# One eight-row pass in place of two diagonal passes for the row of top-2 sums, in an fp32 FFN kernel on one core

## The chip, the core and the metric

The kernel runs on one core of one Trainium2 chip. The metric is the device time of one execution in microseconds; three runs of the kernel before gave 230.13 to 230.21 us, with a median of 230.16 us. The engines are TensorE (PE: matmuls; PEld: its weight loads), VectorE (DVE), ScalarE (ACT), GpSimd (POOL) and SyncE (SP). Each executes its own list of instructions in the order in which they are written, and they meet through semaphores.

## The reference

The input x is 32 x 32 x 512 in fp32, which makes 1024 tokens. Two residual layers are computed. The first runs a grouped convolution with a bias that depends on a condition, then a feed-forward layer whose routed branch is scaled per token by the sum of the two largest gate logits, then a layer norm. The second mixes channels by weights from a small network and applies a dense layer with eight soft-routed low-rank experts. Cut to the lines that the change concerns:

```python
logits = jnp.einsum('bsh,he->bse', hidden_states, gate_w)          # 8 experts
routing_weights, selected_experts = jax.lax.top_k(logits, K)       # K = 2
h = jax.nn.relu(jnp.einsum('bsh,hi->bsi', hidden_states, up_w)) ** 2
shared_out = jnp.einsum('bsi,ih->bsh', h, down_w)
x_latent = jnp.einsum('bsh,hl->bsl', hidden_states, fc1_w)
expert_out = jnp.einsum('bsl,lm->bsm', x_latent, expert_w)
moe_out = expert_out * jnp.sum(routing_weights, axis=-1, keepdims=True)
routed_out = jnp.einsum('bsl,lh->bsh', moe_out, fc2_w)
return _layernorm(shared_out + routed_out, ln_gamma, ln_beta)
```

## The kernel before

The tokens are cut into two halves (h = 0, 1) of four tiles (TPH = 4) of 128 tokens, so that a half is 512 tokens wide, one PSUM bank. There are eight banks: D[0..3] accumulate the output tiles, U[0..1] take the up projection, M[0..1] take everything small. In layer 1 the activations lie with features on the partitions (H_hi, H_lo: the fp32 value cut into two parts that TensorE reads as fp32r), and a product is made of three passes, hi x hi, hi x lo and lo x hi (`mm3`, lines 1121 to 1123).

The order of the work is written out by hand: each engine's block has one list of calls per half. TensorE's list in a half (lines 1363 to 1394) is: convolution, up(0) and up(1) in parts with gate_rows between them (the gate's logits as rows), gate_logits (four small transposes, line 1158), in half 0 also mixing_bias (lines 1359 and 1360), up(2), scale_rows, latent(0), latent(1), then down and up chunks by turns. `up(i)` fills bank U[i % 2]. ScalarE then makes relu of it (line 624), VectorE multiplies the bank by relu (up_square, line 845, semaphore s_sq), ScalarE copies the result to the high part R_hi (up_split, line 630, s_Rh), and VectorE makes the low part R_lo (up_split, line 849, s_R). The down chunks read R_hi and R_lo.

The scale by the top-2 sum must be multiplied into the latent activations, where tokens run along the free dimension. So the four columns of sums (`ssum`, 128 tokens x 4 tiles, one sum per partition) have to become a row of 512 values that stands on all 128 partitions. Before, this is done as follows. `gate_sum` on VectorE finds the two largest logits (line 829), adds them (line 832), rounds the sum to `ssum_hi` (line 835) and keeps the rest in `ssum_lo` (line 837, s_suml). Then VectorE makes `diag_hi`, four 128 x 128 diagonal matrices, by multiplying the identity by each column (line 839, four instructions, s_diag), and ScalarE makes `diag_lo` in the same way from `ssum_lo` (`diag_low`, line 640, four instructions, s_diagl). Both diagonals lie in the buffer lat_hi. TensorE's `scale_rows` waits for both and multiplies a matrix of ones by them in two passes of 512 columns (lines 1184 and 1185):

```python
pe.wait_ge(s_diag, h + 1)
pe.wait_ge(s_diagl, h + 1)
nc.tensor.matmul(M[0], ones_r[:], diag_hi, start=True, stop=False)
nc.tensor.matmul(M[0], ones_r[:], diag_lo, start=False, stop=True).then_inc(s_sbp, 1)
```

ScalarE copies M[0] to `sbc` (`scale_rows`, line 634), and VectorE multiplies the latent banks by it (`lat_scale`, line 856) after `latent(n)`, 12 passes each, has filled them. In half 0, VectorE's list has between gate_sum and up_square(1) the two transposes of `turn_agg` (line 979), and ScalarE's list has `make_B1` (line 700, two copies of what mixing_bias made) behind diag_low. GpSimd meanwhile makes low parts of weights (line 532) and, once turn_agg is done, four copies into BD (line 543).

Of the kernel before, what the change touches and what calls it, by code (L numbers as in the profile page):

```python
# [6 lines left out]
F32 = mybir.dt.float32  # L7
# [9 lines left out]
def bass_adaln_ffn(  # L17
# [85 lines left out]
    with ExitStack() as ctx:  # L103
# [3 lines left out]
        def sem(name):  # L107
            return ctx.enter_context(nc.semaphore(name))
# [42 lines left out]
        ssum = sb("ssum", [P, TPH])  # L151
        ssum_hi = sb("ssum_hi", [P, TPH], F32R)
        ssum_lo = sb("ssum_lo", [P, TPH], F32R)
        st6 = sb("st6", [P, 2, 6])
# [50 lines left out]

        diag_hi, diag_lo = lat_hi[:, 0], lat_hi[:, 1]

# [111 lines left out]
        s_suml = sem("s_suml")  # L319
        s_diag = sem("s_diag")  # L320
        s_diagl = sem("s_diagl")
        s_sbp = sem("s_sbp")
# [179 lines left out]
        def _(pool):  # L502
# [18 lines left out]
                                    ALU.mult).then_inc(s_prod0, 1)  # L521
            nc.gpsimd.memset(nhalf[:], -0.5)
            nc.gpsimd.memset(gate_hl[:].bitcast(mybir.dt.uint32), 0).then_inc(s_gatez, 1)
            nc.gpsimd.memset(BD[:], 0.0).then_inc(s_zero, 1)
# [72 lines left out]
        def _(act):  # L597
# [37 lines left out]

            def diag_low(h):

                act.wait_ge(s_suml, h + 1)
                for t in range(TPH):
                    last = nc.scalar.activation(diag_lo[:, t * P:(t + 1) * P], ident[:], ACT.Copy,  # L640
                                                scale=ssum_lo[:, t:t + 1].bitcast(F32))
                last.then_inc(s_diagl, 1)

            def gate_copy(h):
# [57 lines left out]
            for h in range(HALVES):  # L702
                i0 = h * IC
                if h:
                    for t in range(TPH):
                        split_H(TPH + t)
                up_relu(i0)
                if h == 0:
                    gate_copy(h)
                    up_split(i0)  # L710
                else:
                    up_split(i0)
                    gate_copy(h)
                up_relu(i0 + 1)
                if h == 0:
                    split_dn(0)
                diag_low(h)
                if h == 0:
                    make_B1()
                scale_rows(h)  # L720
                up_split(i0 + 1)
                if h == 0:
                    split_up(5)
                up_relu(i0 + 2)
                up_split(i0 + 2)
                for n in range(LC):
                    if h == 0:
                        split_dn(1 + n)
                        split_up(6 + n)
                    lat_split(h * LC + n)  # L730
                for c in range(3, IC):
                    if h == 0:
                        split_dn(c)
                    up_relu(i0 + c)
                    up_split(i0 + c)
                    if h == 0 and c == 3:
                        act.wait_ge(s_conv, TPH)
                        shift_copies(3)
                    for g in groups_after(h, c):
                        group_split(g)  # L740
# [50 lines left out]
        def _(dve):  # L791
# [29 lines left out]
            def gate_sum(h):  # L821
# [12 lines left out]
                dve.wait_ge(s_sum, h + 1)  # L834
                nc.vector.tensor_copy(ssum_hi[:], ssum[:]).then_inc(s_sumh, 1)
                dve.wait_ge(s_sumh, h + 1)
                nc.vector.tensor_tensor(ssum_lo[:], ssum[:], ssum_hi[:].bitcast(F32), ALU.subtract).then_inc(s_suml, 1)
                for t in range(TPH):
                    last = nc.vector.tensor_scalar(diag_hi[:, t * P:(t + 1) * P], ident[:],
                                                   ssum_hi[:, t:t + 1].bitcast(F32), None, ALU.mult)  # L840
                last.then_inc(s_diag, 1)

# [139 lines left out]
            for h in range(HALVES):  # L982
# [22 lines left out]
                up_square(i0 + 1)  # L1005
                up_split(i0 + 1)
                if h == 0:
                    split_up(5)
# [109 lines left out]
        def _(pe):  # L1118
# [42 lines left out]

            def up(i, part=None):

# [8 lines left out]
                if i >= 2:  # L1172
                    pe.wait_ge(s_R, i - 1)
                for p in range(PH):
                    last = mm3(U[i % 2][:, part], up_hi[:, c, p], up_lo[:, c, p], H_hi[:, p, part],
                               H_lo[:, p, part], p == 0, p == PH - 1)
                if part.stop == TOKH:
                    last.then_inc(s_upp, 1)

            def scale_rows(h):  # L1180

                pe.wait_ge(s_diag, h + 1)
                pe.wait_ge(s_diagl, h + 1)
                nc.tensor.matmul(M[0], ones_r[:], diag_hi, start=True, stop=False)
                nc.tensor.matmul(M[0], ones_r[:], diag_lo, start=False, stop=True).then_inc(s_sbp, 1)

            def latent(n):

                h, c = divmod(n, LC)
                if c == 0:  # L1190
                    pe.wait_ge(s_top, h + 1)
                else:
                    pe.wait_ge(s_sb, h + 1)
# [169 lines left out]
            for h in range(HALVES):  # L1363
# [16 lines left out]
                if h == 0:  # L1380
                    mixing_bias()
                up(h * IC + 2)
                scale_rows(h)
# [70 lines left out]
```

## Time and profile before

| what | value |
|---|---|
| median of 3 runs | 230.16 us (230.13 to 230.21) |
| the profiled execution | span 228.5 us from its first to its last instruction; the page gives no other time of it |
| TensorE busy | 217.1 us, 95% of the span |
| VectorE / ScalarE / GpSimd busy | 134.6 / 85.0 / 62.0 us |
| chain that ended last | TensorE 87%, VectorE 9%, the rest 4% |
| granted TensorE clock, mean | 1.000 |

The span covers the execution's instructions alone; the device time of a run also holds what lies around them, which is why the median is 1.7 us above the span. A matmul row's duration runs from its start to the modelled end of its results, so neighbours overlap; what one costs its engine is the distance from its start to the start of the next.

### The profile page before, as it was taken

Reading aid. Unit: us, or ns where it says so; the run is one execution under the profiler, and the core shown is the slowest. Engines: PE = TensorE matmul, PEld = TensorE weight load, DVE = VectorE, ACT = ScalarE, POOL = GpSimd, SP = SyncE. Lnnn points to the kernel's source line nnn. Section 1 sums busy time; section 2 is a strip of 40 time slices with the busy share of each in tenths; the row PEclk is TensorE's granted clock in tenths of the full one; section 3 lists DMA queues with packets and bytes.
Section 4 is the critical chain, followed back from the end, with each engine's and each line's share of the span. In section 5 each row is a group of like instructions: output and inputs, shape, how many; then the busy total and the mean of one; then the engine's idle time right before and its main releaser. Section 6 shows DMA issues by size and latency. Waiting matters only on the chain.

```text
span 228.5 us, 3173 instructions
## 1 busy us (share of the span) xinstructions
PE 217.1 (95%) x1181; PEld 186.1 (81%) x1181; DVE 134.6 (59%) x279; ACT 85.0 (37%) x165; POOL 62.0 (27%) x72
## 2 busy tenths in 40 slices
PE   2787999999999999999999999999999999999994
PEld 2777886788788888999888888888998998999982
DVE  4998589876943334957462113445997555435442
ACT  6946576745954441123531013442112211211110
POOL 2504022545146643206300002442262220122000
PEclk9999999999999999999999999999999999999999
DMA  5999944200000000007526000000000110110103
GB/s 141 258 392 390 317 59 68 34 0 0 0 3 0 0 0 0 3 0 116 84 35 75 17 3 1 0 0 0 3 0 0 46 49 0 47 46 3 46 4 135
DMA packets 30400, 13.56 MB, mean 59 GB/s; under 512 B 24936, under 2 KB 25512, under 8 KB 30384
## 3 DMA queue, kind: packets, MB, share of 16 engines
q1 hardware_dynamic: 30288, 13.33, 22.2%
q8 instruction: 9, 0.15, 0.3%
q14 instruction: 7, 0.06, 0.1%
q10 hardware_dynamic: 96, 0.03, 0.1%
HBM read 11.26 MB, written 2.10 MB: 58 GB/s over the span
## 4 chain that ended last, share of the span: by engine, by line
PE 87%; DVE 9%; DMA 1%; ACT 1%; issue 0%
PE PS L1121 25%; PE PS L1122 25%; PE PS L1123 24%; PE PS L1133 7%; DVE XS L437 5%; PE PS L1243 3%; DVE up_lo L798 2%; DMA wc_nat<-in_L_cond_weight_dram 1%; DVE H_lo L920 1%; DVE dn_lo L972 0%; ACT fc_hi L690 0%; PE PS L1147 0%; PE PS L1146 0%; PE PS L1272 0%; PE PS L1359 0%
## 5 line engine op out<-in xcount | busy, mean ns | idle before, releaser
L845 DVE TENSOR_TENSOR PS<-PS,relu 128x512 f32<-128x512 f32 x16 | 11.1, 693 | 32.4 <-ACT relu L624 32.4
L1121 PE MATMUL PS<-H_hi,up_hi 128*128 128x512 f32 (+1 forms) x80 | 28.3, 354 | 0.0
L1122 PE MATMUL PS<-H_lo,up_hi 128*128 128x512 f32 (+1 forms) x80 | 27.9, 349 | 0.0
L1123 PE MATMUL PS<-H_hi,up_lo 128*128 128x512 f32 (+1 forms) x80 | 27.8, 347 | 0.0
L1133 PE MATMUL PS<-wconv,XS 128*128 128x128 f32 x192 | 25.0, 295 | 2.0 <-DVE wconv L913 1.5
L1133 PEld LDWEIGHTS PS<-wconv,XS 128*128 128x128 f32 x192 | 24.3, 210 | 2.5 <-DVE wconv L913 1.6
L1121 PE MATMUL PS<-qkT_hi,H_hi 128*128 128x320 f32 x64 | 20.3, 317 | 0.1
L1122 PE MATMUL PS<-qkT_lo,H_hi 128*128 128x320 f32 x64 | 19.8, 309 | 0.0
L1123 PE MATMUL PS<-qkT_hi,H_lo 128*128 128x320 f32 x64 | 19.8, 309 | 0.0
L624 ACT ACTIVATE relu<-PS 128x512 f32<-128x512 f32 x16 | 9.5, 597 | 25.1 <-PE PS L1123 25.1
L570 POOL TENSOR_TENSOR X<-X,rowb 128x512 f32<-128x512 f32 x8 | 10.3, 1288 | 31.3 <-PE PS L1243 31.3
L437 DVE COPY XS<-X 32x128 f32<-32x128 f32 (+2 forms) x40 | 18.1, 454 | 0.5
L1122 PE MATMUL PS<-dn_lo,ring 128*128 128x512 f32 x44 | 17.5, 399 | 0.0
L1121 PE MATMUL PS<-dn_hi,ring 128*128 128x512 f32 x44 | 17.4, 396 | 0.0
L1121 PEld LDWEIGHTS PS<-H_hi,up_hi 128*128 128x128 f32 x80 | 15.1, 189 | 2.7 <-issue 0.4
L1123 PE MATMUL PS<-dn_hi,ring 128*128 128x512 f32 x44 | 17.3, 392 | 0.0
L1123 PEld LDWEIGHTS PS<-H_hi,up_lo 128*128 128x128 f32 x80 | 15.1, 189 | 2.1
L1122 PEld LDWEIGHTS PS<-H_lo,up_hi 128*128 128x128 f32 x80 | 15.1, 189 | 2.0
L438 ACT ACTIVATE XS<-X 32x128 f32<-32x128 f32 (+2 forms) x24 | 15.8, 658 | 0.6 <-DMA X<-in_x_dram 0.3
L532 POOL TENSOR_TENSOR dn_lo<-dn_raw,dn_hi 128x512 fp32r<-128x512 f32 x8 | 10.3, 1289 | 17.2 <-ACT dn_hi L613 17.2
L574 POOL TENSOR_TENSOR wT_lo<-qk_raw,wT_hi 128x512 fp32r<-128x512 f32 x4 | 5.1, 1292 | 36.2 <-ACT wT_hi L658 36.2
L1121 PE MATMUL PS<-wT_hi,H_hi 128*128 128x512 f32 x32 | 13.1, 409 | 0.0
(189 smaller groups left out, 476.5 us busy)
## 6 DMA issues: line engine op xcount, KB each, us to landing
up_raw<-in_L_ffn_up_w_dram SPq DMA_DIRECT2D x2, 1024.0 KB, 8.0
dn_raw<-in_L_ffn_down_w_dram SPq DMA_DIRECT2D x2, 1024.0 KB, 12.9
out_dram<-X SPq DMA_DIRECT2D x8, 256.0 KB, 2.0
X<-in_x_dram SPq DMA_DIRECT2D x1, 1024.0 KB, 15.2
XS<-in_L_ffn_W_dram SPq DMA_DIRECT2D x16, 64.0 KB, 2.3
X<-in_x_dram SPq DMA_DIRECT2D x2, 256.0 KB, 3.4
X<-in_x_dram SPq DMA_DIRECT2D x1, 512.0 KB, 5.4
fc<-in_L_ffn_fc_w_dram SPq DMA_DIRECT2D x1, 512.0 KB, 3.6
```

Of the source, the lines that this page charges most:

```text
L437: return nc.vector.tensor_copy(dst, src)
L438: return nc.scalar.activation(dst, src, ACT.Copy)
L532: nc.gpsimd.tensor_tensor(dn_lo[:, c, :], dn_raw[:, c, :], dn_hi[:, c, :].bitcast(F32), ALU.subtract).then_inc(s_dn, 1)
L570: nc.gpsimd.tensor_tensor(X[:, T, :], X[:, T, :], rowb[:], ALU.add).then_inc(s_x1b, 1)
L574: nc.gpsimd.tensor_tensor(wg_dst(g, False), wg_turned(g), wg_dst(g, True).bitcast(F32), ALU.subtract)\
L624: nc.scalar.activation(relu[:], U[i % 2], ACT.Relu).then_inc(s_relu, 1)
L845: nc.vector.tensor_tensor(U[i % 2], U[i % 2], relu[:], ALU.mult).then_inc(s_sq, 1)
L1121: nc.tensor.matmul(o, lh, rh, start=start, stop=False)
L1122: nc.tensor.matmul(o, lh, rl, start=False, stop=False)
L1123: return nc.tensor.matmul(o, ll, rh, start=False, stop=stop)
L1133: last = nc.tensor.matmul(conv_bank(T)[:, s * P:(s + 1) * P], XS[:, T % TPH * SPT + s, a:a + P], wconv[:, a], start=(a == 0), stop=(a == N ...
L1243: last = nc.tensor.matmul(mix_bank(T)[:, p, :], X[:, T, p * P:(p + 1) * P], BD[:, T], start=True, stop=True)
```

## The change

The sums' high and low parts are put side by side in `ssum_hl`, 128 tokens x 8 columns, both as plain fp32. A new `turn_sums` on TensorE, written between the second and the third of up(2)'s four steps, transposes them into 8 rows of 128 in the bank M[1]. A new `spread_sums` on VectorE, written behind up_split(1), multiplies these 8 rows, repeated four times along the free dimension, by a block mask `blocks` (8 x 4, made once on GpSimd), so that row k keeps only the 128 columns of its own tile; the result `srows` is 8 x 512. `scale_rows` on TensorE then is one pass over 8 rows with 8 rows of ones as weights. The eight diagonal instructions go. ScalarE's up_split(1) stands ahead of its scale_rows now, where it stood behind it. `latent(0)` waits for s_srows instead of s_top.

```diff
-        ssum_hi = sb("ssum_hi", [P, TPH], F32R)
-        ssum_lo = sb("ssum_lo", [P, TPH], F32R)
+        ssum_r = sb("ssum_r", [P, TPH], F32R)
+        ssum_hl = sb("ssum_hl", [P, 2, TPH])
+        blocks = sb("blocks", [2 * TPH, TPH])
...
-        diag_hi, diag_lo = lat_hi[:, 0], lat_hi[:, 1]
+        srows = lat_hi[0:2 * TPH, 0].rearrange("k (t q) -> k t q", t=TPH)
...
             nc.gpsimd.memset(nhalf[:], -0.5)
+            nc.gpsimd.memset(blocks[:], 0.0).then_inc(s_blocks, 1)
+            for i in range(2):
+                pool.wait_ge(s_blocks, i + 1)
+                nc.gpsimd.affine_select(out=blocks[:], in_=blocks[:], compare_op=ALU.not_equal, fill=1.0,
+                                        base=-i * TPH, pattern=[[-1, TPH]], channel_multiplier=1).then_inc(s_blocks, 1)
...
-            def diag_low(h):
-
-                act.wait_ge(s_suml, h + 1)
-                for t in range(TPH):
-                    last = nc.scalar.activation(diag_lo[:, t * P:(t + 1) * P], ident[:], ACT.Copy,
-                                                scale=ssum_lo[:, t:t + 1].bitcast(F32))
-                last.then_inc(s_diagl, 1)
...
                 if h == 0:
                     split_dn(0)
-                diag_low(h)
                 if h == 0:
                     make_B1()
+                up_split(i0 + 1)
                 scale_rows(h)
-                up_split(i0 + 1)
...
-                nc.vector.tensor_copy(ssum_hi[:], ssum[:]).then_inc(s_sumh, 1)
+                nc.vector.tensor_copy(ssum_r[:], ssum[:]).then_inc(s_sumh, 1)
                 dve.wait_ge(s_sumh, h + 1)
-                nc.vector.tensor_tensor(ssum_lo[:], ssum[:], ssum_hi[:].bitcast(F32), ALU.subtract).then_inc(s_suml, 1)
-                for t in range(TPH):
-                    last = nc.vector.tensor_scalar(diag_hi[:, t * P:(t + 1) * P], ident[:],
-                                                   ssum_hi[:, t:t + 1].bitcast(F32), None, ALU.mult)
-                last.then_inc(s_diag, 1)
+                nc.vector.tensor_copy(ssum_hl[:, 0], ssum_r[:].bitcast(F32))
+                nc.vector.tensor_tensor(ssum_hl[:, 1], ssum[:], ssum_r[:].bitcast(F32), ALU.subtract).then_inc(s_suml, 1)
+
+            def spread_sums(h):
+
+                dve.wait_ge(s_sumT, h + 1)
+                dve.wait_ge(s_blocks, 3)
+                nc.vector.tensor_tensor(srows, bcast_mid(M[1][0:2 * TPH, 256:256 + P], TPH),
+                                        blocks[:].unsqueeze(2).broadcast_to([2 * TPH, TPH, P]), ALU.mult)\
+                    .then_inc(s_srows, 1)
...
                 up_square(i0 + 1)
                 up_split(i0 + 1)
+                spread_sums(h)
...
-                pe.wait_ge(s_diag, h + 1)
-                pe.wait_ge(s_diagl, h + 1)
-                nc.tensor.matmul(M[0], ones_r[:], diag_hi, start=True, stop=False)
-                nc.tensor.matmul(M[0], ones_r[:], diag_lo, start=False, stop=True).then_inc(s_sbp, 1)
+                pe.wait_ge(s_srows, h + 1)
+                nc.tensor.matmul(M[0], ones_r[0:2 * TPH, :], lat_hi[0:2 * TPH, 0], start=True, stop=True)\
+                    .then_inc(s_sbp, 1)
+
+            def turn_sums(h):
+
+                pe.wait_ge(s_suml, h + 1)
+                nc.tensor.transpose(M[1][0:2 * TPH, 256:256 + P], ssum_hl[:].rearrange("p v t -> p (v t)"), ident[:])\
+                    .then_inc(s_sumT, 1)
...
                 if c == 0:
-                    pe.wait_ge(s_top, h + 1)
+                    pe.wait_ge(s_srows, h + 1)
...
-                up(h * IC + 2)
+                up(h * IC + 2, ps=range(0, 2))
+                turn_sums(h)
+                up(h * IC + 2, ps=range(2, PH))
                 scale_rows(h)
```

VectorE's list in half 0, from the end of gate_sum on, with what each instruction waits for; lat_hi is the buffer of the diagonals before and of srows now, ring is R_hi and R_lo, and M and U lie in PS. Before:

```order
L835 CAST ssum_hi<-ssum 128x4 [waits s_sum]
L837 TENSOR_TENSOR ssum_lo<-ssum,ssum_hi 128x4 [waits s_sumh]
L839 TENSOR_SCALAR lat_hi<-ident,ssum_hi 128x128 x4
L979 STREAM_TRANSPOSE prod<-PS 32x512 [waits s_AGp]
L979 STREAM_TRANSPOSE prod<-PS 32x512
L845 TENSOR_TENSOR PS<-PS,relu 128x512 [waits s_relu]
L849 TENSOR_TENSOR ring<-PS,ring 128x512 [waits s_Rh]
L798 TENSOR_TENSOR up_lo<-up_raw,up_hi 128x512 [waits s_uph]
```

In the changed kernel (its lines from there on are numbered a few apart):

```order
L833 CAST ssum_r<-ssum 128x4 [waits s_sum]
L835 COPY ssum_hl<-ssum_r 128x4 [waits s_sumh]
L836 TENSOR_TENSOR ssum_hl<-ssum,ssum_r 128x4
L982 STREAM_TRANSPOSE prod<-PS 32x512 [waits s_AGp]
L982 STREAM_TRANSPOSE prod<-PS 32x512
L848 TENSOR_TENSOR PS<-PS,relu 128x512 [waits s_relu]
L852 TENSOR_TENSOR ring<-PS,ring 128x512 [waits s_Rh]
L842 TENSOR_TENSOR lat_hi<-PS,blocks 8x512 [waits s_blocks,s_sumT]
L796 TENSOR_TENSOR up_lo<-up_raw,up_hi 128x512 [waits s_uph]
```

The four instructions that made the diagonals are gone from ahead of the two transposes, and the instruction that the last pass of scale_rows waits for now stands behind up_square(1) and behind up_split(1), which itself waits for ScalarE.

ScalarE's list in half 0, from up_relu(1) on. Before:

```order
L624 ACTIVATE relu<-PS 128x512 [waits s_sq,s_upp]
L613 ACTIVATE dn_hi<-dn_raw 128x512 [waits ld_dn0]
L640 ACTIVATE lat_hi<-ident,ssum_lo 128x128 [waits s_suml]
L640 ACTIVATE lat_hi<-ident,ssum_lo 128x128 x3
L700 ACTIVATE B<-PS 128x512 [waits s_B1p] x2
L634 ACTIVATE sbc<-PS 128x512 [waits s_sbp]
L630 ACTIVATE ring<-PS 128x512 [waits s_sq]
L609 ACTIVATE up_hi<-up_raw 128x512 [waits ld_up1]
L624 ACTIVATE relu<-PS 128x512 [waits s_sq,s_upp]
```

In the changed kernel:

```order
L631 ACTIVATE relu<-PS 128x512 [waits s_sq,s_upp]
L620 ACTIVATE dn_hi<-dn_raw 128x512 [waits ld_dn0]
L699 ACTIVATE B<-PS 128x512 [waits s_B1p] x2
L637 ACTIVATE ring<-PS 128x512 [waits s_sq]
L641 ACTIVATE sbc<-PS 128x512 [waits s_sbp]
L616 ACTIVATE up_hi<-up_raw 128x512 [waits ld_up1]
L631 ACTIVATE relu<-PS 128x512 [waits s_sq,s_upp]
```

The copy to the ring (up_split(1)) no longer stands behind the copy to sbc, and the diagonals are gone from ahead of both.

TensorE's list in half 0 around scale_rows; the rows with up_hi and up_lo are steps of up(2), the rows with fc_hi are latent(0). Before:

```order
L1121 MATMUL PS<-H_hi,up_hi 128x512
L1122 MATMUL PS<-H_lo,up_hi 128x512
L1123 MATMUL PS<-H_hi,up_lo 128x512
L1184 MATMUL PS<-lat_hi,ones_r 128x512 [waits s_diagl,s_diag]
L1185 MATMUL PS<-lat_hi,ones_r 128x512
L1121 MATMUL PS<-H_hi,fc_hi 128x512 [waits s_fc,s_top]
```

In the changed kernel:

```order
L1127 MATMUL PS<-H_hi,up_lo 128x512
L1193 MATMUL PS<-ident,ssum_hl 8x128 [waits s_suml]
L1125 MATMUL PS<-H_hi,up_hi 128x512 [waits s_R,s_up]
L1126 MATMUL PS<-H_lo,up_hi 128x512
L1127 MATMUL PS<-H_hi,up_lo 128x512
L1125 MATMUL PS<-H_hi,up_hi 128x512
L1126 MATMUL PS<-H_lo,up_hi 128x512
L1127 MATMUL PS<-H_hi,up_lo 128x512
L1187 MATMUL PS<-lat_hi,ones_r 128x512 [waits s_srows]
L1125 MATMUL PS<-H_hi,fc_hi 128x512 [waits s_fc,s_srows]
```

The wait for s_srows stands at the one pass of scale_rows, and the whole of latent(0) and latent(1) is queued behind it.

## Rows read from the trace of the kernel before

**Rows 1.** The page, part 1: the span, and TensorE's busy time and instructions.
```profile
span 228.5 us, 3173 instructions
...
PE 217.1 (95%) x1181; PEld 186.1 (81%) x1181; DVE 134.6 (59%) x279; ACT 85.0 (37%) x165; POOL 62.0 (27%) x72
```

**Rows 2.** The page, part 4: the chain that ended last, by engine.
```profile
PE 87%; DVE 9%; DMA 1%; ACT 1%; issue 0%
```

**Rows 3.** Waits of TensorE (us in total, times, longest us); five rows in all.
```profile
PE PS L1313 <- DVE H_lo L920: 1.9, 1, 1.9
...
PE PS L1359 <- DVE dn_lo L972: 0.2, 1, 0.2
```

**Rows 4.** Timeline, TensorE, first half (start us, us busy, engine, line, [idle before]).
```profile
39.14 0.49 PE L1359 MATMUL PS<-dn_lo,ones_r 8*128 8x512 f32 x1 [0.17 <-DVE dn_lo L972]
39.47 0.38 PE L1360 MATMUL PS<-dn_lo,ones_r 8*128 8x512 f32 x1
...
41.75 0.39 PE L1121 MATMUL PS<-H_hi,up_hi 128*128 128x512 f32 x1
...
43.12 0.39 PE L1184 MATMUL PS<-lat_hi,ones_r 128*128 128x512 f32 x1
...
43.58 0.40 PE L1121 MATMUL PS<-H_hi,fc_hi 128*128 128x512 f32 x1
```

**Rows 5.** Timeline, VectorE, first half.
```profile
41.39 0.16 DVE L837 TENSOR_TENSOR ssum_lo<-ssum,ssum_hi 128x4 fp32r<-128x4 f32 x1
41.47 0.87 DVE L839 TENSOR_SCALAR lat_hi<-ident,ssum_hi 128x128 fp32r<-128x128 f32 x4
42.25 1.29 DVE L979 STREAM_TRANSPOSE prod<-PS 32x512 f32<-32x512 f32 x2
43.48 0.66 DVE L845 TENSOR_TENSOR PS<-PS,relu 128x512 f32<-128x512 f32 x1
44.89 0.69 DVE L849 TENSOR_TENSOR ring<-PS,ring 128x512 fp32r<-128x512 f32 x1 [0.75 <-ACT ring L630]
...
48.60 1.42 DVE L798 TENSOR_TENSOR up_lo<-up_raw,up_hi 128x512 fp32r<-128x512 f32 x1 [0.35 <-ACT up_hi L609]
```

**Rows 6.** Timeline, ScalarE, first half.
```profile
41.59 1.28 ACT L640 ACTIVATE lat_hi<-ident,ssum_lo 128x128 fp32r<-128x128 f32 x4 [1.81 <-DVE ssum_lo L837]
42.77 1.05 ACT L700 ACTIVATE B<-PS 128x512 f32<-128x512 f32 x2
```

**Rows 7.** Timeline, GpSimd, first half.
```profile
43.69 3.12 POOL L543 COPY BD<-prod 32x256 f32<-32x256 f32 x4 [2.55 <-DVE prod L979]
```

**Rows 8.** Timeline, VectorE, second half.
```profile
106.77 0.70 DVE L845 TENSOR_TENSOR PS<-PS,relu 128x512 f32<-128x512 f32 x1 [0.34 <-ACT relu L624]
108.13 0.69 DVE L849 TENSOR_TENSOR ring_last<-PS,ring_last 128x512 fp32r<-128x512 f32 x1 [0.67 <-ACT ring_last L630]
...
110.98 0.87 DVE L839 TENSOR_SCALAR lat_hi<-ident,ssum_hi 128x128 fp32r<-128x128 f32 x4
111.77 0.69 DVE L845 TENSOR_TENSOR PS<-PS,relu 128x512 f32<-128x512 f32 x1
```

**Rows 9.** Timeline, ScalarE, second half.
```profile
107.50 0.60 ACT L630 ACTIVATE ring_last<-PS 128x512 fp32r<-128x512 f32 x1 [0.77 <-DVE PS L845]
```

**Rows 10.** Timeline, TensorE, second half.
```profile
112.53 0.48 PE L1184 MATMUL PS<-lat_hi,ones_r 128*128 128x512 f32 x1
...
113.07 0.39 PE L1121 MATMUL PS<-H_hi,fc_hi 128*128 128x512 f32 x1
```

**Rows 11.** TensorE's transposes of line 1272 (duration ns min/median/max).
```profile
L1272 PE MATMUL PS<-ident,hw x8: 270/271/273, 172.9 to 223.4; 128*128 128x128 f32 x8
```

**Rows 12.** Busy time in stretches: us, PE, PEld, DVE, ACT, POOL busy (instructions), PEclk, DMA.
```profile
7.30:12.80 5.50, 5.47 (x24) 5.20 (x24) 5.36 (x11) 5.38 (x10) 3.38 (x4) 1.00 0.95 271
13.30:16.10 2.80, 2.80 (x24) 2.80 (x25) 2.70 (x8) 0.64 (x1) 0.00 (x0) 1.00 1.04 399
18.60:19.60 1.00, 1.00 (x4) 0.84 (x5) 0.65 (x2) 0.00 (x0) 1.00 (x1) 1.00 1.04 385
```

More of the change, by code:

```diff
@@ L319, in bass_adaln_ffn @@
         s_suml = sem("s_suml")
-        s_diag = sem("s_diag")
-        s_diagl = sem("s_diagl")
+        s_sumT = sem("s_sumT")
+        s_srows = sem("s_srows")
+        s_blocks = sem("s_blocks")
         s_sbp = sem("s_sbp")
@@ L1160, in gate_logits, with up @@
                 last.then_inc(s_gp, 1)
-            def up(i, part=None):
+            def up(i, part=None, ps=range(PH)):
                 h, c = divmod(i, IC)
@@ L1173, in up @@
                     pe.wait_ge(s_R, i - 1)
-                for p in range(PH):
+                for p in ps:
                     last = mm3(U[i % 2][:, part], up_hi[:, c, p], up_lo[:, c, p], H_hi[:, p, part],
                                H_lo[:, p, part], p == 0, p == PH - 1)
-                if part.stop == TOKH:
+                if part.stop == TOKH and p == PH - 1:
                     last.then_inc(s_upp, 1)
             def scale_rows(h):
-                pe.wait_ge(s_diag, h + 1)
-                pe.wait_ge(s_diagl, h + 1)
-                nc.tensor.matmul(M[0], ones_r[:], diag_hi, start=True, stop=False)
-                nc.tensor.matmul(M[0], ones_r[:], diag_lo, start=False, stop=True).then_inc(s_sbp, 1)
+                pe.wait_ge(s_srows, h + 1)
[5 more added lines that the diff above has]
+                    .then_inc(s_sumT, 1)
             def latent(n):
```

## The prediction

> **What bounds the kernel now.** I read the page's first part, then the chain, then the waits of TensorE, then timelines. TensorE is busy for 217.1 of 228.5 us [rows 1], and the chain that ended last runs over it for 87% [rows 2]. Of the five rows of its waits the last in time is 0.2 us before line 1359, at 39.14 us [rows 3, 4]; from there to the end nothing that the profile shows holds it up. So a microsecond that TensorE loses behind 39 us is a microsecond of the end, and so is one that it saves. Work taken from VectorE and ScalarE is worth nothing by itself, unless TensorE waits for it. The question is therefore what the change takes from TensorE's list, and at what time VectorE now hands over what scale_rows waits for.
>
> **What the change removes on TensorE.** The two passes and what they begin with take 43.58 - 43.12 = 0.46 us in the first half [rows 4] and 113.07 - 112.53 = 0.54 us in the second [rows 10]. One of them goes; the other stays, since eight rows of 512 columns are no shorter in the trace than 128 rows: line 1359 and its neighbour, eight rows each, stand 0.33 us apart where the first had waited [rows 4]. That 0.33 us is what I take for the single pass, which now has a wait in front.
>
> **What it adds on TensorE.** One transpose per half, 128 columns in fp32. Below, a plain fp32 pass of 128 columns costs 2.80 / 24 = 0.12 us of the list [rows 12]; above, a whole transpose lasts 0.27 us [rows 11], and with its weights not loaded ahead I take 0.3 us. It waits for s_suml. VectorE starts a new copy of 128 x 4 where the subtraction started, at 41.39 us, and the subtraction 0.08 us later, by the distance from 41.39 to 41.47; so that ends near 41.63 us [rows 5]. TensorE reaches the transpose at 41.75 us, the start of up(2)'s third step [rows 4]. It hardly waits. TensorE would then be ready for scale_rows at 43.12 + 0.3 = 43.4 us.
>
> **When the rows are there, first half.** VectorE's list decides it, since spread_sums stands behind turn_agg, up_square(1) and up_split(1). The diagonals held the list from 41.47 to 42.25 us, that is 0.78 us, and go; the new copy gives 0.08 us back. So turn_agg starts at 41.55 instead of 42.25 us, and up_square(1), 43.48 - 42.25 = 1.23 us behind it, at 42.78; with 0.66 us it ends at 43.44 us [rows 5]. ScalarE is free by then: it made B1 only at 42.77 us because it stood behind the diagonals, four instructions in 1.28 us [rows 6], and what B1 copies is ready before 41.75 us, when TensorE is far into up(2) [rows 4]. The step from square to ring copy to low part is shown undisturbed in the second half: the square ends at 107.47 us, the copy starts at 107.50 with 0.60 us, the subtraction at 108.13 with 0.69 us [rows 8, 9]. So here: ring copy 43.48 to 44.08, subtraction 44.11 to 44.80. Spread_sums starts 0.08 us before the end of the instruction ahead of it, at 44.72 us.
>
> Its own duration the trace doesn't show. The nearest rows read one operand of 512 elements from PSUM and one from SBUF: 0.66 and 0.69 us [rows 5]. Below, I see none shorter than 0.66 for 512 elements. Above, the slowest VectorE instruction of that width took 1.42 us [rows 5]; both its inputs lay in SBUF. I take 0.67 us, since spread_sums too reads PSUM, and the square at 43.48 and the subtraction at 44.89 us ran at their usual pace although GpSimd copied from 43.69 us for 3.12 us beside them [rows 5, 7]. The Trainium skill, "SBUF — State Buffer", section "SBUF: two separate sides", says the same in general: VectorE is locked out by GpSimd when it reads two SBUF inputs or runs in a two-port mode, and not otherwise. By a lock for any VectorE instruction, which the page denies, the sum would be 0.75 us higher in the first half.
>
> So the rows are there at 45.39 us, and a pass that waits for VectorE starts about 0.06 us behind it, as at 39.14 us; scale_rows runs at 45.45 and latent(0) at 45.78 us, where it started at 43.58 us. TensorE stands still for 45.45 - 43.4 = 2.0 us, and the first half loses **2.20 us** in all. The removed pass and the added transpose don't enter: whatever TensorE saves or spends ahead of that wait is taken out of the wait.
>
> **Second half.** There is no turn_agg. The diagonals held VectorE from 110.98 to 111.77 us; without them and with the copy, up_square(9) starts at 111.77 - 0.79 + 0.08 = 111.06 and ends at 111.75 us [rows 8]. Ring copy 111.79 to 112.39, subtraction 112.42 to 113.11, spread_sums 113.03 to 113.70 us. Scale_rows starts at 113.76, latent(0) at 114.09 us instead of 113.07 [rows 10]: **1.02 us** lost, of which 0.9 us is standing still.
>
> **What is behind the waits.** ScalarE's copy to sbc waits for scale_rows, and behind it are up_hi(5) and relu(2). They come later by less than TensorE does, since up_split(1) is already out of their way; VectorE's next squares follow them. I cost them at nothing: latent(0) and latent(1) cover them, 24 passes of 0.23 us. If that cover were gone, down(2) would wait for up(2)'s low part. The block mask on GpSimd is made some 30 us ahead of its use and costs nothing; nothing is added to a DMA queue.
>
> **Sum.** 2.20 + 1.02 = 3.2 us on the profiled span of 228.5 us gives 231.7 us. The runs lie 1.7 us above that span, so the median goes from 230.16 to **233.4 us**, 1.4% slower. A measurement of this kernel can tell about 0.2%, or 0.46 us, from no change.
>
> **The rivals.**
> 1. *The rows come in time (229.8 to 230.2 us), not slower.* If spread_sums ended before TensorE arrives, the list alone would count: minus two passes of 0.23 us, minus 0.08 us for the wait that line 1184 shows in the second half (0.54 against 0.46), plus two transposes of 0.12 to 0.3 us: -0.3 to +0.06 us. It decides at an end of spread_sums by 43.4 us in the first half, 2.0 us earlier than I get. For it speaks that the chain of VectorE to the sums themselves is done by 41.63 us; against it the hand-written place behind two instructions of VectorE and one of ScalarE, 3.2 us of work. Chance 4%.
> 2. *The first stall is absorbed (231.2 us).* If TensorE had slack later that the profile doesn't show, only the second half's 1.02 us would be left. Against it: no wait in the rows behind 39 us [rows 3]. Chance 6%.
> 3. *The clock falls in the stall (236.1 us).* 24 passes of 128 columns took 5.47 us early in the kernel, after standing still, and the same 24 took 2.80 us at 13.3 us [rows 12]: half the pace, although the granted clock is printed as 1.00 for both. One such stretch after the 2.0 us stall costs 2.67 us more. Against it: after the wait of 1.9 us before line 1313 [rows 3] four passes of 512 columns take 1.00 us, the full pace of 2.4 GHz [rows 12]. Chance 9%. The Trainium skill, "TensorE: Matmul & The Clock Gate", section "HAM oscillation — how this bites in real kernels", has the rule that speaks against the change: gaps in TensorE's work can send the clock from 2.4 to 1.2 GHz, and what follows starts slow. The trace neither shows it for a gap of this size nor excludes it for a slightly longer one.
>
> **How the numbers follow.** The forecast has 81%. Its own range: -0.6 us if TensorE's weight load and the semaphores hide 0.15 us at two waits and the steps of VectorE are 0.15 us shorter per half, +1.5 us if spread_sums takes its upper bound of 1.42 us in both halves. That is 232.8 to 234.9 us; I widen the low end to 232.5 us for a stall that is partly absorbed. The range 232.5 to 234.9 holds about 8 in 10, since rivals 1 to 3, 19%, lie outside. Faster by over 0.2%: half of rival 1, 2%. Within 0.2%: its other half and a sixth of rival 2, 3%. Slower: 95%.
>
> **What would show it.** In the changed profile TensorE's waits should hold two new entries, before the single pass of scale_rows, of 2.0 and 0.9 us with VectorE's spread as the releaser, and the spread at 44.7 and about 2.2 us later than today's clock, 115.2 us, in the second half, lasting 0.67 us. The transpose should cost 0.12 to 0.3 us and hardly wait. The distance from up(2)'s last step to latent(0) should be 2.2 and 1.0 us longer; everything behind it shifted by just that. The prediction is wrong if no such wait is there, if a later wait of TensorE shrinks, or if passes after the stall are 0.4 us apart instead of 0.23.

## The result and the profile after

The changed kernel takes 232.86 us, the median of ten runs (231.95 to 235.32), beside 230.2 us for the kernel before in the same comparison (230.03 to 231.76). The ratio is 1.0096, with a 95% interval of 1.0067 to 1.0126: slower, by 2.2 us (1.5 to 2.9), where 3.2 us had been forecast. The ratio puts it at 232.4 us, 0.1 us under the stated range; the median of 232.86 us by itself lies inside it. The direction was right and the size too large.

One thing must be known to read the times. Each kernel here falls into separate levels, and each run's mean granted TensorE clock tells which. Of 82 runs of the kernel before that stood beside the runs below, 47 had a clock of 1.00 and a median of 230.11 us, and 35 had 0.993 and 231.77 us. The changed kernel has three levels: five runs at 232.14 us (clock 0.997 to 1.0), four at 233.69 (0.991 to 0.993) and one at 235.32 (0.985). Level against level, the change costs 2.0 us (1.9 us in the second level). The profiled execution is one of the middle level.

The page of it:

```profile
span 232.0 us, 3167 instructions
...
PE 217.1 (94%) x1181; PEld 186.1 (80%) x1181; DVE 134.6 (58%) x275; ACT 82.9 (36%) x157; POOL 62.2 (27%) x75
```

TensorE is busy for as long as before, 217.1 us, so the span grew by what it stood still; that its work took the same time is a balance of slower and faster passes, as the rows below show. Its waits (us in total, times, longest us):

```profile
PE PS L1187 <- DVE lat_hi L842: 2.9, 2, 2.0
PE PS L1322 <- DVE H_lo L923: 2.0, 1, 2.0
```

The first row is the new one: two waits, 2.0 and 0.9 us, for VectorE's spread. The second is the older pause, 1.9 us in the kernel before [rows 3]. The timeline of TensorE in the first half (start us, us busy) answers [rows 4]:

```profile
41.69 0.27 PE L1193 MATMUL PS<-ident,ssum_hl 128*8 128x128 f32 x1
41.72 0.47 PE L1125 MATMUL PS<-H_hi,up_hi 128*128 128x512 f32 x1
...
42.96 0.40 PE L1127 MATMUL PS<-H_hi,up_lo 128*128 128x512 f32 x1
45.35 0.68 PE L1187 MATMUL PS<-lat_hi,ones_r 8*128 8x512 f32 x1 [2.00 <-DVE lat_hi L842]
45.96 0.80 PE L1125 MATMUL PS<-H_hi,fc_hi 128*128 128x512 f32 x1
46.55 0.63 PE L1126 MATMUL PS<-H_lo,fc_hi 128*128 128x512 f32 x1
46.98 0.63 PE L1127 MATMUL PS<-H_hi,fc_lo 128*128 128x512 f32 x1
...
49.26 0.40 PE L1127 MATMUL PS<-H_hi,fc_lo 128*128 128x512 f32 x1
49.50 0.39 PE L1125 MATMUL PS<-H_hi,fc_hi 128*128 128x512 f32 x1
```

The transpose and its neighbour start at 41.69 and 41.72 us; nothing waits there. The pass of scale_rows starts at 45.35 us. From 46.55 us on the passes of latent(0) stand 0.43 us apart, until they return to 0.23 us by 49.26 us. VectorE in the same stretch, for [rows 5]:

```profile
41.40 0.16 DVE L836 TENSOR_TENSOR ssum_hl<-ssum,ssum_r 128x4 f32<-128x4 f32 x1
...
42.70 0.66 DVE L848 TENSOR_TENSOR PS<-PS,relu 128x512 f32<-128x512 f32 x1
44.02 0.69 DVE L852 TENSOR_TENSOR ring<-PS,ring 128x512 fp32r<-128x512 f32 x1 [0.66 <-ACT ring L637]
44.63 0.67 DVE L842 TENSOR_TENSOR lat_hi<-PS,blocks 8x512 fp32r<-8x512 f32 x1
```

Spread_sums, the last row, starts at 44.63 us and lasts 0.67 us. The whole program up to here is 0.07 us earlier than before, and with that the forecast's 44.72 and 45.39 us are met within 0.02 us. The second half of TensorE, for [rows 10]:

```profile
115.56 0.39 PE L1127 MATMUL PS<-H_hi,up_lo 128*128 128x512 f32 x1
116.85 0.49 PE L1187 MATMUL PS<-lat_hi,ones_r 8*128 8x512 f32 x1 [0.90 <-DVE lat_hi L842]
117.27 0.50 PE L1125 MATMUL PS<-H_hi,fc_hi 128*128 128x512 f32 x1
117.61 0.39 PE L1126 MATMUL PS<-H_lo,fc_hi 128*128 128x512 f32 x1
```

Here the clock is full, and the distances from the pass of scale_rows to latent(0) and on to its second pass are 0.42 and 0.34 us. The granted clock (PEclk, the value behind GpSimd's count in brackets) in two stretches of the first half:

```profile
45.96:48.69 2.73, 2.73 (x8) 2.15 (x7) 1.30 (x2) 1.74 (x4) 0.00 (x0) 0.50 0.03 9
49.00:53.00 4.00, 4.00 (x19) 3.27 (x18) 2.81 (x4) 1.90 (x5) 1.29 (x1) 1.00 0.00 0
```

At 0.50 TensorE has 1.2 GHz of its 2.4 GHz: eight passes touch the 2.73 us from 45.96 us on, nineteen the 4 us from 49 us on.

### The profile page after: what moved, and what is told of

It reads as the page before. It is cut to its first block, busy times and chain, and to the rows that moved or that the text cites. A ratio compares the mean times of both kernels' runs of the same rounds, so it can differ in the third digit from the quotient of the medians.

```text
span 232.0 us, 3167 instructions
## 1 busy us (share of the span) xinstructions
PE 217.1 (94%) x1181; PEld 186.1 (80%) x1181; DVE 134.6 (58%) x275; ACT 82.9 (36%) x157; POOL 62.2 (27%) x75
## 4 chain that ended last, share of the span: by engine, by line
PE 83%; DVE 12%; ACT 1%; DMA 1%; issue 1%
PE PS L1125 24%; PE PS L1126 23%; PE PS L1127 23%; PE PS L1137 7%; DVE XS L439 5%; PE PS L1252 3%; DVE up_lo L796 2%; DMA wc_nat<-in_L_cond_weight_dram 1%; DVE PS L848 1%; DVE lat_hi L842 1%; DVE H_lo L923 1%; ACT ring L637 1%; DVE prod L982 1%; PE PS L1187 1%; DVE ssum L830 1%
## 5 line engine op out<-in xcount | busy, mean ns | idle before, releaser
L1137 PE MATMUL PS<-wconv,XS 128*128 128x128 f32 x192 | 24.3, 291 | 2.5 <-DVE wconv L916 1.5
L1137 PEld LDWEIGHTS PS<-wconv,XS 128*128 128x128 f32 x192 | 23.8, 206 | 3.0 <-DVE wconv L916 1.6
```

The costliest lines, as they stand in the source:

```text
L1137: last = nc.tensor.matmul(conv_bank(T)[:, s * P:(s + 1) * P], XS[:, T % TPH * SPT + s, a:a + P], wconv[:, a], start=(a == 0), stop=(a == N ...
```

## The experiments

The times of the kernel before, the changed kernel and 14 others, by the level of the clock. The ratio in the last column is over all runs of a kernel, whatever their level, so a kernel that stays in its first level gains a little there by that alone. Within one level the runs of a kernel lie up to 0.6 us apart (e10_warm7: 228.01 to 228.60 us), so a difference of 0.2 us between two medians says nothing. "Ring" is the byte at which that buffer starts in each partition in the compiled program, modulo 256.

| kernel | ring | clock 0.995 and up: runs, median | 0.988 to 0.993: runs, median | 0.985: runs, median | ratio (95%) |
|---|---|---|---|---|---|
| before | 160 | 47, 230.11 | 35, 231.77 | none | 1 |
| changed | 192 | 5, 232.14 | 4, 233.69 | 1, 235.32 | 1.0096 (1.0067 to 1.0126) |
| e1_pad32 | 192 | 5, 228.58 | 7, 230.24 | none | 0.9935 (0.9906 to 0.9965) |
| e2_unshift | 128 | 2, 233.11 | 1, 234.78 | 3, 236.36 | 1.0174 (1.0118 to 1.0230) |
| e3_early | 192 | 8, 229.12 | 4, 230.73 | none | 0.9939 (0.9910 to 0.9967) |
| e4_pad64 | 224 | 7, 229.61 | 5, 231.17 | none | 0.9973 (0.9942 to 1.0004) |
| e5_same_addr | 160 | 1, 233.75 | 4, 235.26 | 1, 236.71 | 1.0172 (1.0129 to 1.0215) |
| e6_fill_late | 192 | 4, 232.09 | 6, 233.69 | none | 1.0093 (1.0058 to 1.0127) |
| e7_pad32_warm | 192 | 6, 229.24 | none | none | 0.9908 (0.9872 to 0.9943) |
| e9_rows8 | 192 | 9, 229.10 | 3, 230.98 | none | 0.9936 (0.9905 to 0.9967) |
| e10_warm7 | 192 | 6, 228.41 | none | none | 0.9908 (0.9880 to 0.9936) |
| e11_early_warm7 | 192 | 9, 229.12 | none | none | 0.9932 (0.9906 to 0.9957) |
| e12_pad_mid | 160 | 5, 229.51 | 7, 231.14 | none | 0.9995 (0.9966 to 1.0024) |
| e13_pad96 | 0 | 4, 227.56 | 2, 229.29 | none | 0.9889 (0.9851 to 0.9926) |
| e14_after_warm7 | 192 | 3, 231.96 | 4, 233.56 | none | 1.0103 (1.0066 to 1.0139) |
| e15_pad96_warm7 | 0 | 6, 227.38 | none | none | 0.9862 (0.9829 to 0.9894) |

### Where 1.6 us came back: the place of the buffers

Laying the two executions side by side, pass by pass, showed a lag of 3.8 us at 49 us that shrank to 3.1 us at 90 us, grew by the second wait to 4.3, and shrank again to 3.6 us at 160 us. In those stretches each 512-column pass took less time than before. The change declares 32 bytes more of small tiles (three where there were two, 32 bytes each at least), so that everything behind them lies 32 bytes further on.

e1_pad32, the kernel before with nothing but that shift:

```diff
         ssum_lo = sb("ssum_lo", [P, TPH], F32R)
+        pad = sb("pad", [P, 8])
```

> The kernel before with 32 unused bytes per partition behind ssum_lo, so that every later buffer (ring, lat_hi, the second layer's weights) moves by the 32 bytes by which the change moves them; H, up and dn stay. No instruction differs. Theory A (the addresses set the pace of TensorE's 512-column passes): three passes of a product cost 226 + 229 + 232 ns as in the changed kernel instead of 231 + 231 + 238, the stretch from 49 us to the end shortens by about 1.6 us, the time is 228.6 us. Theory B (the pause sets the pace that follows): nothing changes, 230.2 us.

Measured: 228.58 us at the full clock, 1.53 us under the kernel before. The counts of instructions in two stretches of 20 us, in the kernel before:

```profile
60.00:80.00 20.00, 20.00 (x88) 16.16 (x87) 9.67 (x16) 10.64 (x15) 10.11 (x8) 1.00 0.00 1
130.00:150.00 20.00, 20.00 (x88) 16.17 (x87) 6.73 (x11) 5.52 (x10) 3.83 (x3) 1.00 0.00 1
```

and in e1_pad32:

```profile
60.00:80.00 20.00, 20.00 (x90) 16.46 (x89) 10.16 (x16) 11.95 (x16) 9.71 (x8) 1.00 0.00 1
130.00:150.00 20.00, 20.00 (x90) 16.47 (x89) 6.57 (x11) 5.44 (x9) 3.83 (x3) 1.00 0.01 1
```

TensorE is busy all the time in both, with 88 passes before and 90 here. From the starts in the traces, the down passes of the first half stand 233.5 ns apart before and 229.2 ns in e1_pad32, the up passes 230.2 and 226.7 ns; the changed kernel has the numbers of e1_pad32. Theory A holds.

e2_unshift, the changed kernel with the shift undone:

```diff
-        ssum_r = sb("ssum_r", [P, TPH], F32R)
-        blocks = sb("blocks", [2 * TPH, TPH])
...
         bT_lo = sb("bT_lo", [P, L], F32R)
+        ssum_r = sb("ssum_r", [P, TPH], F32R)
+        blocks = sb("blocks", [2 * TPH, TPH])
```

> The changed kernel with ssum_r and blocks allocated behind all other buffers, so that ring, lat_hi and the rest stand where they stood before the change. No instruction differs from the changed kernel. Theory A: the pauses of 2.0 and 0.9 us are paid in full, the pace falls back to 231/231/238 ns, about 1.6 us slower than the changed kernel: 233.7 us where TensorE's clock is not turned down, 235.3 us where it is. Theory B: the same as the changed kernel, 232.1 and 233.7 us.

Measured: 233.11 us, and down passes at 232.9 ns. But the edit did not do what its expectation says: each small tile takes 32 bytes, so ring moved to 128 instead of back to 160. e5_same_addr adds 32 unused bytes and puts it right:

```diff
         ssum_hl = sb("ssum_hl", [P, 2, TPH])
+        pad = sb("pad", [P, 8])
```

> The changed kernel with ssum_r and blocks behind all other buffers and 32 unused bytes in their old place. Every tile takes at least 32 bytes, so the kernel of the run e2_unshift had moved ring, lat_hi and the rest 32 bytes down instead of back; here they stand exactly where they stood in the kernel before (ring at byte 167584). If the addresses set the pace, the down passes go back to 231/231/238 ns and the lowest level is that of the kernel before plus the two pauses and what the new passes cost, 230.1 + 3.3 = 233.4 us, with 1.6 us more for each time that the clock is turned down. If something else in the changed kernel gave the pace, the lowest level is 232.1 us.

Measured: 233.75 us for the one run at the full clock, 235.26 and 236.71 for the others, so 3.6 us above the kernel before at the full clock and 3.5 us in the next level. A single run is little, but the trace says the same: against the trace of before, TensorE's list falls back by 2.34 us around up(2) and the start of latent(0) in the first half (transpose, wait and 8-row pass together), by 1.23 us in the second, 3.57 us in all, and nowhere else. The counts are those of before:

```profile
60.00:80.00 20.00, 20.00 (x88) 16.15 (x87) 10.72 (x17) 12.63 (x16) 7.97 (x7) 1.00 0.00 1
130.00:150.00 20.00, 20.00 (x88) 16.15 (x87) 5.89 (x9) 4.30 (x8) 1.29 (x1) 1.00 0.00 1
```

This is the change with nothing of the shift in it.

e4_pad64 has `[P, 16]` in the place of e1_pad32's `[P, 8]`, e13_pad96 `[P, 24]`:

> The kernel before with 64 unused bytes in the same place. Theory A: another pace again, of which I only know that it lies between some 226 and 233 ns per pass, 228.6 to 230.5 us. Theory B: 230.2 us.

> The kernel before with 96 unused bytes ahead of ring (ring then starts at a multiple of 256 bytes). Paces of the down passes so far: 233.5 ns for ring at 160 above a multiple of 256, 229.2 at 192, 233.2 at 224, 232.9 at 128. If the pace repeats every 128 bytes, this one is as 128 above: 232.9 ns and 229.7 us; if alignment to 256 helps, 229 ns and 228.6 us.

Measured: 229.61 us for 64 bytes, with down passes at 233.2 and up passes at 226.6 ns; 227.56 us for 96 bytes, where every product of the first layer runs at 226.6 ns. So the pace does not repeat every 128 bytes (ring at 128 and at 0 differ by 6 ns a pass), and the start at a multiple of 256 is the best of the five. In all of them the operands that stream past the weights (dn, ex, H) stayed where they were, so no run tells whether the place of the weights counts by itself or by its distance from theirs. The same two stretches of e13_pad96:

```profile
60.00:80.00 20.00, 20.00 (x90) 16.57 (x89) 10.39 (x17) 12.10 (x17) 9.63 (x8) 1.00 0.00 1
130.00:150.00 20.00, 20.00 (x90) 16.56 (x89) 6.79 (x11) 5.59 (x10) 3.83 (x3) 1.00 0.00 1
```

e12_pad_mid asks which buffer matters; the 32 bytes lie between ring (slots 0 and 1 of R_hi and R_lo) and ring_last (slot 2):

```diff
+        pad = sb("pad", [P, 8])
         with ExitStack() as later:
```

> The kernel before with the 32 unused bytes placed behind ring instead of ahead of it: relu and the ring's slots 0 and 1 stand where they stood, ring_last (slot 2), lat_hi, lat_lo and the second layer's weights move by 32 bytes. If a pass's own weights' address sets its pace, the down chunks that read slot 2 and the routed passes run at 229 ns a pass, the down chunks on slots 0 and 1 at 233.5, and the time lies between, near 229.5 us. If relu's or the ring's place sets it for all, everything stays at 233.5 and 230.2 ns and 230.1 us.

Measured: 229.51 us, and a pace that changes inside one half. The first passes of four chunks of twelve, of TensorE:

```profile
65.61 0.39 PE L1122 MATMUL PS<-dn_hi,ring_last 128*128 128x512 f32 x1
...
68.36 0.39 PE L1122 MATMUL PS<-H_hi,up_hi 128*128 128x512 f32 x1
...
71.09 0.39 PE L1122 MATMUL PS<-dn_hi,ring 128*128 128x512 f32 x1
...
73.89 0.40 PE L1122 MATMUL PS<-H_hi,up_hi 128*128 128x512 f32 x1
```

Twelve down passes with weights from ring_last take 68.36 - 65.61 = 2.75 us, 229 ns each; twelve with weights from ring take 73.89 - 71.09 = 2.80 us, 233 ns each. The routed passes (weights from the moved lat_hi and lat_lo) ran at 229.3 ns. For down and routed passes the place of their own weights sets the pace. Up passes, whose operands all stayed put, ran at 226.6 ns behind a chunk on slot 2 and at 230.2 ns behind one on slots 0 and 1 (228.5 ns behind the routed passes): they take over something from the passes ahead of them. It fades: in the chunk at 73.89 us the first eight distances are 224 to 236 ns, the last three 226 or 227. And it is not the pace itself, since in e4_pad64 up passes ran at 226.6 ns behind down passes at 233.2. What it is, and why 32 bytes matter, no run here shows.

### What the 8-row pass costs

e3_early moves spread_sums to where the rows are in time:

```diff
                 if h == 0:
                     turn_agg()
+                    spread_sums(h)
                 up_square(i0 + 1)
+                if h:
+                    spread_sums(h)
                 up_split(i0 + 1)
-                spread_sums(h)
```

> The changed kernel with spread_sums moved: in the first half behind the two transposes of turn_agg and ahead of up_square(1), in the second half ahead of up_split(9). The rows should be there at 43.4 us, as TensorE arrives. Both waits before scale_rows fall to under 0.3 us, the clock is never turned down, the second value of time disappears. Theory A: addresses as in the changed kernel, so 228.6 to 229.0 us, faster than before. Theory B: without the pause the old pace comes back, 230.0 to 230.4 us.

Measured: 229.12 us, and neither wait stands in the list of TensorE's waits any more. The second level did not disappear, so it is not of the change's making alone. With the same layout e1_pad32 has 228.58 us, 0.5 us less: without its pauses the change still costs something. The timeline shows where, in the first half:

```profile
42.86 0.40 PE L1129 MATMUL PS<-H_hi,up_lo 128*128 128x512 f32 x1
43.30 0.49 PE L1189 MATMUL PS<-lat_hi,ones_r 8*128 8x512 f32 x1
43.72 0.50 PE L1127 MATMUL PS<-H_hi,fc_hi 128*128 128x512 f32 x1
44.06 0.39 PE L1128 MATMUL PS<-H_lo,fc_hi 128*128 128x512 f32 x1
```

Up(2)'s last pass, the 8-row pass and latent(0)'s first two. From first to last 1.20 us, where four evenly spaced passes take 0.69 us. Of that about 0.1 us is a last wait for VectorE, which ends the spread at 43.24 us.

e9_rows8 puts an 8-row pass into e1_pad32 in the place of the second diagonal pass; it leaves out most of the low parts of the sums:

```diff
-                nc.tensor.matmul(M[0], ones_r[:], diag_lo, start=False, stop=True).then_inc(s_sbp, 1)
+                nc.tensor.matmul(M[0], ones_r[0:8, :], diag_lo[0:8], start=False, stop=True).then_inc(s_sbp, 1)
```

> The kernel of e1_pad32 with the second pass of scale_rows over 8 rows instead of 128 (it leaves out the low parts of all but the first eight tokens of each tile), nothing else. It measures the 8-row pass by itself. If rows don't matter to TensorE, as I took it in the prediction, the lowest level stays at 228.55 us. If a change of the number of rows keeps TensorE from loading the next weights beside the running pass, as the gap of 0.42 and then 0.34 us behind the pass in the run e3_early suggests, it is 0.3 to 0.4 us slower per half: 229.2 to 229.4 us.

Measured: 229.10 us, 0.52 us above e1_pad32 and 0.69 us above e10_warm7 (below), which has the same layout. TensorE's passes, then its weight loads:

```profile
43.03 0.40 PE L1185 MATMUL PS<-lat_hi,ones_r 128*128 128x512 f32 x1
43.36 0.49 PE L1186 MATMUL PS<-lat_hi,ones_r 8*128 8x512 f32 x1
43.78 0.50 PE L1122 MATMUL PS<-H_hi,fc_hi 128*128 128x512 f32 x1
44.12 0.39 PE L1123 MATMUL PS<-H_lo,fc_hi 128*128 128x512 f32 x1
```

```profile
42.90 0.19 PEld L1185 LDWEIGHTS PS<-lat_hi,ones_r 128*128 128x128 f32 x1
43.36 0.18 PEld L1186 LDWEIGHTS PS<-lat_hi,ones_r 8*128 8x128 f32 x1 [0.28 <-issue]
43.78 0.19 PEld L1122 LDWEIGHTS PS<-H_hi,fc_hi 128*128 128x128 f32 x1 [0.24 <-issue]
43.89 0.19 PEld L1123 LDWEIGHTS PS<-H_lo,fc_hi 128*128 128x128 f32 x1
```

The distances around the 8-row pass are 0.33, 0.42 and 0.34 us, together 0.40 us more than three times 0.23. Beside the trace of e1_pad32 it is 0.39 us in each half, 0.78 us in all, more than the 0.52 us between the medians; the difference is within what runs of one kernel differ by. Its weights are loaded only at 43.36 us, when it starts, and the next 128-row weights at 43.78 us, when their pass starts; between passes of 128 rows each load starts a pass ahead, as the last row does for the pass at 44.12 us.

### What turns the clock down

The older pause shows its step in e1_pad32, whose profiled execution is of the second level. TensorE stood still for 1.9 us until 18.36 us; then:

```profile
19.80:23.20 3.40, 3.40 (x18) 3.40 (x17) 3.20 (x6) 2.63 (x4) 0.66 (x1) 0.50 1.05 401
23.20:24.80 1.60, 1.60 (x17) 1.60 (x16) 0.74 (x2) 0.00 (x0) 0.00 (x0) 1.00 1.04 387
```

The granted clock is 0.50 in the first stretch, with 18 instructions of TensorE in 3.4 us, where e9_rows8, at the full clock, has 33.

e6_fill_late fills the change's two pauses with passes whose result is overwritten, e14_after_warm7 fills the older pause before line 1313's passes [rows 3] and leaves the change's two:

```diff
                 up(h * IC + 2, ps=range(2, PH))
+                for _ in range(3 if h else 8):
+                    nc.tensor.matmul(M[0], ones_r[:], H_hi[:, 0], start=True, stop=True)
                 scale_rows(h)
```

```diff
             pe.wait_ge(s_ones, 2)
+            for _ in range(7):
+                nc.tensor.matmul(D[3][:, 0:P], XS[:, 0, 0:P], wconv[:, 0], start=True, stop=True)
             pe.wait_ge(s_prod0s, 1)
```

> The changed kernel with passes of 512 columns that fill the pauses before scale_rows, eight in the first half and three in the second (0.23 us each, into the bank M[0] that scale_rows then overwrites; work that the reference does not ask for). They end before the rows are there, so no wait gets longer. If the pause of 2.0 us is what turns the clock down at 45 us, that never happens here: two levels are left, 232.1 and 233.7 us (the early pause before line 1313's passes), and no run at 235.3. If the pause has nothing to do with it, the three levels stay.

> The changed kernel with the early pause filled by the 7 passes of e10_warm7; only the change's own pauses before scale_rows are left. If the pause of 2.0 us in the first half turns the clock down by itself, two levels are left, 232.1 and 233.7 us, and the profile of a slow one shows the granted clock at 0.50 from about 45 us. If it doesn't, every run lies at 232.1 us, and all of the changed kernel's spread came from the early pause.

Their waits, e6_fill_late first:

```profile
PE PS L1322 <- DVE H_lo L923: 1.9, 1, 1.9
...
PE PS L1187 <- DVE lat_hi L842: 0.2, 1, 0.2
```

```profile
PE PS L1187 <- DVE lat_hi L842: 2.9, 2, 2.0
...
PE PS L1324 <- DVE H_lo L923: 0.3, 1, 0.3
```

With either pause alone there are two levels and no run at the third: four and six runs of e6_fill_late, three and four of e14_after_warm7. (The profiled execution of e14_after_warm7 is one at the full clock; the clock at 0.50 behind the late pause is seen in the changed kernel's profile above.) With both pauses (the changed kernel, e2_unshift, e5_same_addr) 5 of 22 runs have the third. With neither, as below, all 27 runs have the full clock. Each pause of about 2 us turns the clock down in roughly half of the runs (35 of 82 of before, 4 of 7 of e14_after_warm7), which costs about 1.6 us each time; no run of any kernel has more steps down than the kernel has pauses of that length, so the one of 0.9 us gave none in the 29 runs that have it.

e7_pad32_warm and e10_warm7 are e1_pad32 with 14 and 7 of those filling passes:

> The kernel before with the 32 unused bytes of e1_pad32, and with 14 passes of 128 columns written into TensorE's pause before line 1313's passes (16.7 to 18.4 us; 14 x 0.115 = 1.6 us, into D[3] ahead of the convolution that overwrites it). If that pause of 1.9 us is what gives the kernel before its second level (231.6 us beside 230.1), the second level disappears: all runs at 228.5 to 228.6 us, 1.6 us under the low level of before, and this is the fastest kernel of the study. If not, levels at 228.55 and 230.2 us stay.

> The kernel of e7_pad32_warm with 7 filling passes instead of 14: a plain fp32 pass is two instructions of 0.115 us in the trace, so the 14 ran for 3.2 us and held TensorE up past the pause. Seven last 1.6 us and fit into it. If the pause before line 1313's passes gives the second level of time, all runs lie at 228.5 to 228.7 us with a clock of 0.997 or more. If filling shortens nothing, levels at 228.6 and 230.2 us come back.

Fourteen were too many (a plain fp32 pass is two instructions, which I had counted as one) and delayed line 1313's passes, at 229.24 us; seven leave 0.3 us of the pause:

```profile
PE PS L1316 <- DVE H_lo L921: 0.3, 1, 0.3
```

All six runs are at the full clock, with a median of 228.41 us. e11_early_warm7 is e3_early with the same seven:

> The kernel of e3_early (the change with spread_sums placed early) with the same 7 filling passes. All runs at one level, at 229.1 us: 0.5 us above e10_warm7, which has the two diagonal passes, if the 8-row pass costs TensorE more than the pass that it replaces; at 228.5 us or below if it doesn't.

All nine are at the full clock, with a median of 229.12 us, 0.7 us above e10_warm7. In the traces, TensorE's list falls back against e10_warm7 by 0.12 and 0.18 us at the two transposes, and the rest around the 8-row passes, 0.74 us in all. Placed well and measured beside the same layout and clock, the change loses to the two diagonal passes. And the two findings without the change, e13_pad96 with the seven passes:

> The kernel before with the 96 unused bytes of e13_pad96 and the 7 filling passes: the two things that the study found, together, with the two diagonal passes kept. All runs at one level, 227.4 to 227.8 us, 2.6 us under the low level of before and 5.5 us under the changed kernel's median.

227.38 us, the fastest of the study: 1.4% (1.1 to 1.7%) under all runs of the kernel before, and 1.2% under those of them at the full clock.

## Why the prediction was wrong

**What held.** The bound (TensorE's list), the removed and added instructions, the chain on VectorE with its 0.67 us for the spread, both waits (2.0 and 0.9 us, forecast 2.0 and 0.9), the transpose that hardly waits, and the cover for what ScalarE does behind. GpSimd's copies did not hold the spread up, as the rows and the Trainium skill, "SBUF — State Buffer", section "SBUF: two separate sides", had it: in the changed kernel they ran from 42.91 us for 2.64 us, and the spread beside them took 0.67 us.

**Mis-sized: the single pass.** The step "eight rows of 512 columns are no shorter" took 0.33 us to the next pass, from line 1359 [rows 4], and 0.23 us behind it. Measured: 0.42 and 0.34 us, 0.2 us more in each half. The row that I used has another 8-row pass behind it; what costs is the step from 128 rows to 8 and back. The forecast of 3.2 us with 2 x 0.2 us is the 3.6 us of e5_same_addr, where only the change is left. The Trainium skill, "TensorE: Matmul & The Clock Gate", section "Step-by-step: what each phase is for", says that TensorE pulls a weight load ahead of running passes when the row groups don't conflict or the background buffer takes it, and that the number of rows doesn't change a load's time. The loads agree in length (0.18 and 0.19 us); that none is pulled ahead beside the 8-row pass is what the rows of e9_rows8 show.

**Missing: the buffers' place.** The step that failed is the sum's silent last term, "everything behind it shifted by just that". The diff shows three small tiles in place of two; I read them as free. They moved every later buffer by 32 bytes, and with that the 512-column passes became faster by about 4 ns each, 1.53 us in e1_pad32 and 233.75 - 232.14 = 1.6 us between e5_same_addr and the changed kernel. It is nearly half of what the change itself loses, and no part of its idea. Without it the changed kernel would have lain inside the range: e5_same_addr, at 1.0172 times the kernel before, has 234.2 us.

**Rival 3, the clock.** It had 9% and came true for the new pause in about half of the runs (4 of 7 of e14_after_warm7, where no other pause of that length is left), at 1.6 us instead of 2.67 us, since the half pace lasted shorter than the 5.47 us that I had priced: in the profile, from behind 45.35 us to about 48.7 us. The evidence against it was one execution of before in which the clock stayed up after the pause of 1.9 us; over many runs the same pause turns it down in 35 of 82. The three runs that gave the 230.16 us, at 230.13 to 230.21 us, were by their times all of the first level. The Trainium skill, "TensorE: Matmul & The Clock Gate", section "HAM oscillation — how this bites in real kernels", has gaps send the clock to 1.2 GHz; the trace agrees, with the clock at 0.50 behind the pause, though the gaps of the page's example are longer than the 2.0 us here. How often it happens, one profile cannot show. Rivals 1 and 2 did not occur: no later wait shrank.

The levels then come out as 230.11 + 3.2 + 0.4 - 1.5 = 232.2 us at the full clock, measured 232.14, with the 1.5 us from e1_pad32, and 1.6 us more for each step down. That the median of 232.86 us came within 0.6 us of the forecast is in part luck: a gain that I had not seen was partly made up by two losses, one sized too small and one given 9%.

## What to carry to other kernels

Before an instruction that TensorE waits for is moved down another engine's list, add up what stands ahead of it there; here 3 us of VectorE and ScalarE work stood ahead of a row that was needed at once, and the place alone cost 3.0 us (232.14 against 229.12 us of e3_early). A declaration of a few bytes can be worth more than the edit it belongs to: compare a change with the old kernel at the same buffer addresses, and try several starts of the weights' buffers; here a multiple of 256 bytes was the best of five. A pause of 2 us on TensorE costs more than itself in about half of the runs, and idle passes written into it are a cheap cure if they end before the pause does.

## What was not expected of the hardware

- The pace of a 512-column fp32r pass depends on where its weights lie: 226.6 ns for a down pass with ring at a multiple of 256 bytes, 229.2 with ring 192 bytes above one, 232.9 to 233.5 with 128, 160 or 224 above. Up passes, whose own operands never moved, ran at 226.6, 229.5 or 230.2 ns, depending on where the weights of the passes ahead of them lay. The cause stays open.
- A pass over 8 rows between passes over 128 rows costs 0.4 us more than a 128-row pass in its place (e9_rows8, in each half).
- The same pause of about 2 us lets the granted clock fall to 0.50 in about half of the runs: 35 of 82 of the kernel before, none of 27 where it was filled.
